# First attention of a two-layer kernel: projections as three fp32r products, the choice of experts one step later, the loop written out

## The chip, the cores and the metric

The kernel runs on one core of one Trainium2 chip. The metric is the device time of one execution in microseconds; less is better. The engines are named as the profile names them: PE (TensorE, matmuls), PEld (its weight loads), DVE (VectorE), ACT (ScalarE), POOL (GpSimd) and SP (SyncE, which only issues DMAs here).

## What is computed

The reference runs a transformer of two layers on x of 8 rows of 256 tokens with 128 features. Each layer has an attention and a feed-forward part, both behind a layer norm whose scale and shift come from a small conditioning vector. The change concerns the first attention and what follows it up to the experts' lists:

```python
h = _layernorm(x) * (1 + ca) + sa
q = (h @ w_q), kv = (h @ w_kv)          # 16 heads of 64: 128 -> 1024 columns
q, kv = rotated by position; q *= scale
# local keys: windows of 128 with the window before; global keys: softmax-pooled segments of 16
attn = softmax([global scores, local scores]); out = attn @ v
x = x + ga * (out @ w_out + b_out)
h = _layernorm(x) * (1 + cb) + sb
topk_vals, topk_idx = top_k(h @ router_w, 2)     # 4 experts
# the experts of layer 0 (fp32, 2730 hidden columns), then layer 1: another attention, 16 experts
```

## The kernel before, in words

Four stages run one after the other: layer0_attention, layer0_experts, layer1_attention, layer1_experts. Only the first is changed. It ends at about 590 us of the span.

**The pipeline of rows.** layer0_attention works on the 8 batch rows in steps that the code calls slots, from -2 to 8. In slot s the heads of row s are computed (`heads`), while row s+2 is normalised and its keys are projected and rotated (`norm`), row s+1 gets its key statistics, pooled segments and transposed keys (`early`), and row s-1 its output projection, residual, second layer norm, router and choice of experts (`late`). `parts` says which of these a slot has: slots 2 to 5 have all. Within a slot the loop runs over hp, 0 to 7, one pair of heads each ("pair 0" to "pair 7" below). Every engine has its own program of the same shape, slot_program, and all waits are written out by hand with semaphores. over_slots writes slots -2 to 1 and 6 to 8 out and puts slots 2 to 5 into a hardware loop of two turns.

**The heads.** For each pair PE computes the scores of pair n (L493 adds the mask, L498 the products), then the query projection of pair n+1 (q_proj, L481), then the attention-value product of pair n-2 (av, L526, L530) and the transposes of the probabilities of pair n-1 (pT_tr, L512, L514). DVE takes the reciprocal of the sums (L1021), the maximum of the scores (L1025), and rotates the queries of pair n+1 (L1081, L1085). ACT normalises the probabilities of pair n-1 (L648), takes the exponentials of pair n (L638), and copies the results of PE out (L701, L707, L708). A row's first scores wait for all its transposed keys, which ACT copies in pairs 6 and 7 (L661).

**What stands between them.** Pair 0: DVE reduces the logits (L851), centres keys (L835) and takes the statistics of the first layer norm of row s+2 (layernorm1, L761 to L769); PE transposes the logits at its end. Pair 1: segment softmax. Pair 2: on DVE segment_weights, kv_variance (L844, L846) and residual (L920 to L940); on PE the output projection (L539); POOL raises the variance to -0.5 (key_rstd, L1138) as soon as L846 is done, and then does weigh (L1160), normalise (L1147) and scale_keys (L1153). Pair 3: layernorm1_end (L806). Pair 4: PE transposes n2 and h (L547, L424), ACT writes hkv (L680) and h2T (L687), PE pools the segments (G_mm, L454) and projects the keys of half a row (kv_mm, L431); pair 5: the other half, the router matmul (L554), and on DVE pooled_variance (L903), kv_cosine (L818), router_rows (L950) and choose (L960 to L982), the choice of two experts for each token. Pair 6 and 7: rotation of the keys (L825, L827, L818 on DVE, L1127 and L1134 on POOL), key transposes (L471). At the end of pair 7 PE counts the places of row s-1 in the experts' lists (pos_mm, L562, L563), DVE makes them into indices (list_places, L987 to L1006), ACT copies hkv to hT (L737), and POOL scatters the rows to the lists with four indirect DMAs (L1230).

**The banks.** A0 and A1 are two PSUM banks that many small steps share. A string fixes the order of their uses in each slot, and each use waits until the one before is read out.

**Operands.** The projections are fp32 matmuls, each of which the trace shows as two records (PE) of two passes. The weights wq and wkv lie in SBUF as fp32, hT and hkv too. modb holds all six modulation vectors of every row, broadcast to 128 partitions.

## Time and profile before

| | |
|---|---|
| median of 3 runs | 1512.7 us (1509.84 to 1518.84) |
| profiled execution | 1513.62 us, span 1511.8 us |
| mean granted clock of TensorE | 0.896 |
| PE busy | 1200.5 us (79%) |
| DVE busy | 931.4 us (62%) |
| ACT busy | 822.3 us (54%) |
| POOL busy | 725.5 us (48%) |
| first scores of slot 0 | at 81.67 us |
| first rows read by the experts' stage | 594.35 us |

A timeline row of the profile has the start in us, the time in us from the first to the last of the merged instructions, the engine, the line, the operation with what it writes and reads, and their count; in brackets stands how long the engine was idle before and what ended that. A matmul's end is modelled with its way through the array, so a record's duration is longer than its distance to the next. The granted clock (PEclk) is 1.00 at 2.4 GHz and 0.50 at 1.2 GHz. A row of busy times has the stretch, its length, then busy us and, in parentheses, the instructions of PE, PEld, DVE, ACT and POOL, then PEclk, the share of the DMA engines and GB/s.

### The profile page before, as it was taken

To read this page: it belongs to the slowest core of one execution; us is meant where nothing else is said; L and a number is where in the kernel's file an instruction comes from. 1 tells how busy PE (TensorE), PEld (TensorE's weight loads), DVE (VectorE), ACT (ScalarE), POOL (GpSimd) and SP (SyncE) were. 2 spreads that over 40 slices of the span, in tenths; PEclk is the share of its full clock that TensorE was granted. 3 is DMA by queue.
4 is the path that set the end of the run, shared out by engine and by line. 5 is a ranking of instruction groups with operands and counts; after the bars stand their busy time and mean duration, and the time that the engine had idled before them with its cause. 6 is when DMAs were issued, how large, how long until landed. Compare 5 with 4: busy or idle time off the path is not lost. (4 is left out here: it accounts for less than half of the span.)

```text
span 1511.8 us, 30131 instructions
## 1 busy us (share of the span) xinstructions
PE 1200.5 (79%) x9299; PEld 928.5 (61%) x9299; DVE 931.4 (62%) x2122; ACT 822.3 (54%) x2181; POOL 725.5 (48%) x750
## 2 busy tenths in 40 slices
PE   3368988989889993898899899889937887888436
PEld 1245665656656662898899889889913444444336
DVE  4687787787876533744744664764434677776633
ACT  1256777767677771676676666666612443344101
POOL 2646748567485312565566556556653323211223
PEclk8589999989998995999999999999966999899558
DMA  7500000000000003303003000000063445331145
GB/s 221 174 2 3 1 10 3 8 10 0 9 2 8 10 8 127 124 11 125 8 11 120 16 9 10 12 12 7 10 174 81 84 87 104 58 48 21 23 121 152
DMA packets 152775, 76.43 MB, mean 51 GB/s; under 512 B 99992, under 2 KB 143384, under 8 KB 152408
## 3 DMA queue, kind: packets, MB, share of 16 engines
q1 hardware_dynamic: 144696, 66.42, 16.8%
q0 software_dynamic: 3072, 6.31, 1.3%
q10 hardware_dynamic: 4896, 2.36, 0.5%
q8 instruction: 54, 0.88, 0.2%
q14 instruction: 57, 0.47, 0.1%
HBM read 54.77 MB, written 19.76 MB: 49 GB/s over the span
## 5 line engine op out<-in xcount | busy, mean ns | idle before, releaser
L1477 POOL TENSOR_TENSOR hl<-hid,hh 128x256 fp32r<-128x256 f32 x396 | 294.0, 744 | 218.8 <-ACT hh L1454 215.1
L1520 DVE SCALAR_TENSOR_TENSOR hid<-GU,gub,sg 128x256 f32<-128x256 f32 x396 | 190.5, 482 | 194.7 <-ACT sg L1448 123.5
L1348 PE MATMUL GU<-xh,wh 128*128 128x256 f32 x792 | 233.3, 295 | 39.4 <-DVE wl L1496 30.3
L1448 ACT ACTIVATE sg<-GU,gub 128x256 f32<-128x256 f32 x396 | 188.1, 475 | 123.6 <-PE GU L1350 121.7
L1349 PE MATMUL GU<-xl,wh 128*128 128x256 f32 x792 | 225.3, 284 | 0.0
L1350 PE MATMUL GU<-xh,wl 128*128 128x256 f32 x792 | 225.1, 284 | 0.0
L1348 PEld LDWEIGHTS GU<-xh,wh 128*128 128x128 f32 x792 | 152.1, 192 | 49.0 <-issue 27.3
L1454 ACT CAST hh<-hid 128x256 fp32r<-128x256 f32 x396 | 158.2, 399 | 25.8 <-DVE hid L1520 25.3
L1349 PEld LDWEIGHTS GU<-xl,wh 128*128 128x128 f32 x792 | 152.5, 193 | 0.0
L1350 PEld LDWEIGHTS GU<-xh,wl 128*128 128x128 f32 x792 | 152.2, 192 | 0.0
L648 ACT ACTIVATE prob<-prob,rZ 128x272 f32<-128x272 f32 (+1 forms) x256 | 98.9, 462 | 60.6 <-DVE rZ L1021 55.2
L1961 ACT ACTIVATE pT<-ST 128x1024 f32<-128x1024 f32 x64 | 65.5, 1024 | 106.1 <-PE ST L1791 100.9
L1348 PE MATMUL OUT<-hh,wh 128*128 128x256 f32 x396 | 113.5, 287 | 10.8 <-ACT yT L1420 9.8
L2084 DVE TENSOR_REDUCE top_now<-S 128x4 f32<-128x1024 f32 x64 | 78.3, 1223 | 58.8 <-PE S L1783 50.6
L638 ACT ACTIVATE prob<-S,negmax 128x272 f32<-128x272 f32 (+1 forms) x256 | 106.6, 426 | 12.1 <-DVE negmax L1025 11.8
L1349 PE MATMUL OUT<-hl,wh 128*128 128x256 f32 x396 | 111.8, 282 | 0.0
L1350 PE MATMUL OUT<-hh,wl 128*128 128x256 f32 x396 | 111.7, 282 | 0.0
L1025 DVE TENSOR_REDUCE negmax<-S 128x2 f32<-128x544 f32 (+1 forms) x128 | 69.1, 581 | 67.7 <-PE S L498 64.6
L1783 PE MATMUL S<-KA,QA 32*128 32x256 f32 x512 | 81.2, 439 | 11.1 <-DVE top_now L2084 8.1
L1348 PEld LDWEIGHTS OUT<-hh,wh 128*128 128x128 f32 x396 | 75.3, 190 | 14.4 <-POOL hl L1477 13.6
L1138 POOL TENSOR_TENSOR krs<-krs,half 128x32 f32<-128x32 f32 x8 | 43.9, 5491 | 80.2 <-DVE krs L846 80.2
L1791 PE MATMUL ST<-QA,KA 32*128 32x256 f32 x512 | 78.8, 428 | 0.0
(312 smaller groups left out, 2842.6 us busy)
## 6 DMA issues: line engine op xcount, KB each, us to landing
raw<-in_expert_w SPq DMA_DIRECT2D x4, 2688.0 KB, 12.0
late<-in_w SPq DMA_DIRECT2D x20, 256.0 KB, 6.1
raw<-in_expert_w SPq DMA_DIRECT2D x4, 1152.0 KB, 6.1
list<-zero SPq DMA_DIRECT2D x4, 1024.0 KB, 8.6
modb<-mod_d SPq DMA_DIRECT2D x9, 384.0 KB, 4.3
early<-rel_d SPq DMA_DIRECT2D x1, 3072.0 KB, 13.1
qkv_d<-qkv SPq DMA_DIRECT2D x48, 64.0 KB
early<-in_w SPq DMA_DIRECT2D x12, 256.0 KB, 4.2
```

The source lines that it names most:

```text
L638: act.activation(prob[:, hp % 2, prob_at(t, e):prob_at(t, e) + KEYS[t]], S[:, e, S_AT[t]:S_AT[t] + KEYS[t]], ACT.Exp, bias=negmax[:, hp % ...
L648: i = act.activation(part, part, ACT.Copy, scale=rZ[:, pb, t, e:e + 1])
L1348: pe.matmul(out, lhs[0], rhs[0], start=start, stop=False, skip_group_check=True)
L1349: pe.matmul(out, lhs[0], rhs[1], start=False, stop=False, skip_group_check=True)
L1350: return pe.matmul(out, lhs[1], rhs[0], start=False, stop=stop, skip_group_check=True)
L1448: act.activation(sg[:, c % BUFS], GU[c % BUFS][:, 0:TT], ACT.Silu, bias=gub[:, GATE, e * CH0 + c:e * CH0 + c + 1]).then_inc(silu, 1)
L1454: act.copy(hh[:, d % BUFS], hid[:, d % BUFS]).then_inc(hid_hi, 1)
L1477: pool.tensor_tensor(hl[:, b], hid[:, b], hh[:, b].bitcast(F32), ALU.subtract).then_inc(hid_lo, 1)
L1520: dve.scalar_tensor_tensor(out=hid[:, c % BUFS], in0=GU[c % BUFS][:, TT:2 * TT], scalar=gub[:, UP, e * CH0 + c:e * CH0 + c + 1], in1=sg[:, ...
L1783: mm = pe.matmul(S[:, e, blk * NT:(blk + 1) * NT], QA[32 * j:32 * j + BLOCK, row % 2, g, blk * P:(blk + 1) * P], KA[32 * j:32 * j + BLOCK, ...
L1791: mm = pe.matmul(ST[:, e, blk * NT:(blk + 1) * NT], KA[32 * j:32 * j + BLOCK, row % 2, g, blk * P:(blk + 1) * P], QA[32 * j:32 * j + BLOCK ...
L2084: dve.tensor_reduce(to, S[:].rearrange("p e (q k) -> p e q k", q=2), X, ALU.max, negate=True).then_inc(s_max, 1)
```

## The change

Three things are done at once.

- **Split operands.** wq, wkv and the normalised input are each kept as a high part rounded to fp32r and a low part, the difference. A projection is three fp32r matmuls, high*high, high*low and low*high, into one accumulation (three), in place of one fp32 matmul. ACT makes the high parts (of wkv ahead of the slots, of wq in slot -1, of the input in pair 4 beside hkv), DVE the low ones (wkvl in slot -2, wql in slot -1, input_low in pair 4). The copy of hkv to hT goes. The fp32 weights share the memory of attT and pT.
- **One row later.** choose for row s-2 runs in pair 1 of slot s, its exponential on ACT there too, list_places and pos_mm in pair 2, the scatters at the head of the next slot, with two buffers for h2 and slot_now. pos_mm and its operands are bf16. The statistics of layernorm1 move from pair 0 to pair 4 of the slot before. A slot 9 is added for the last row's choice. The order in bank 0 has pos behind lgT.
- **Loops written out.** over_slots has no hardware loop any more, nor has SP's pooled_values. modb holds three of the six vectors.

```diff
@@ over_slots, parts @@
-def over_slots(eng, slot_program):
-    slot_program(-2, 0)
...
-    with eng.Fori(0, 2) as j:
-        slot_program(2 * j + 2, 0)
-        slot_program(2 * j + 3, 1)
-    for slot in range(6, NB + 1):
+def over_slots(slot_program):
+    for slot in range(-2, NB + 2):
         slot_program(slot, slot % 2)
@@ tiles @@
-        wq = sb("wq", [P, 2, INNER])
-        wkv = sb("wkv", [P, INNER])
+        wqh = sb("wqh", [P, 2, INNER], F32R)
+        wql = sb("wql", [P, 2, INNER], F32R)
+        wkvh = sb("wkvh", [P, INNER], F32R)
+        wkvl = sb("wkvl", [P, INNER], F32R)
-        modb = sb("modb", [P, NB, 6 * D])
+        modb = sb("modb", [P, NB, 3 * D])
-        hT = sb("hT", [P, 2, NT])
+        hTh = sb("hTh", [P, 3, NT], F32R)
+        hTl = sb("hTl", [P, 3, NT], F32R)
+        wq = attT[:].rearrange("p c q -> p (c q)").rearrange("p (s n) -> p s n", s=2)
+        wkv = pT[:].rearrange("p a e q -> p (a e q)")[:, 0:INNER]
-        h2 = sb("h2", [P, TILES, D])
+        h2 = sb("h2", [P, 2, TILES, D])
-        both = sb("both", [P, TILES, E0])
-        seen = sb("seen", [P, TILES + 1, E0])
+        both = sb("both", [P, TILES, E0], BF16)
+        seen = sb("seen", [P, TILES + 1, E0], BF16)
-        slot_now = sb("slot_now", [P, 2, TILES], U32)
+        slot_now = sb("slot_now", [P, 2, 2, TILES], U32)
-        bank0 = Bank(..., "lgT:E out:L h2T:L G:E kv00:N kv10:N kT1:E kT3:E pos:L")
+        bank0 = Bank(..., "lgT:E pos:M out:L h2T:L G:E kv00:N kv10:N kT1:E kT3:E")
@@ PE @@
+            def three(out, lhs, rhs):
+                pe.matmul(out, lhs[0], rhs[0], start=True, stop=False, skip_group_check=True)
+                pe.matmul(out, lhs[0], rhs[1], start=False, stop=False, skip_group_check=True)
+                return pe.matmul(out, lhs[1], rhs[0], start=False, stop=True, skip_group_check=True)
             def kv_mm(slot, t, n):
+                b = slot + 2
                 if t == 0 and n == 0:
-                    bank1.wait_emptied(pe, "hT", slot)
+                    pe.wait_ge(hq, b + 1)
+                    pe.wait_ge(w_low, 1)
                 bank, a = use(f"kv{t}{n}", slot)
-                pe.matmul(a[:], hkv[:, t * P:(t + 1) * P], wkv[:, n * 512:(n + 1) * 512],
-                          start=True, stop=True).then_inc(bank.full, 1)
+                tokens, cols = slice(t * P, (t + 1) * P), slice(n * 512, (n + 1) * 512)
+                three(a[:], (hTh[:, b % 3, tokens], hTl[:, b % 3, tokens]), (wkvh[:, cols], wkvl[:, cols])).then_inc(bank.full, 1)
             def q_proj(n, b, bp, hp):
                 if hp == 0:
                     pe.wait_ge(hq, b + 1)
+                    pe.wait_ge(w_low, 2)
...
                 for s in range(2):
-                    mm = pe.matmul(Q[:, s * NT:(s + 1) * NT], wq[:, s, hp * P:(hp + 1) * P], hT[:, bp, :],
-                                   start=True, stop=True)
+                    mm = three(Q[:, s * NT:(s + 1) * NT], (wqh[:, s, cols], wql[:, s, cols]), (hTh[:, b % 3, :], hTl[:, b % 3, :]))
             def pos_mm(slot, b):
-                    pe.matmul(a[:, t * E0:(t + 1) * E0], cst("before"), both[:, t, :], start=True, stop=False)
-                    mm = pe.matmul(a[:, t * E0:(t + 1) * E0], cst("ones"), seen[:, t, :], start=False, stop=True)
+                    pe.matmul(a[:, t * E0:(t + 1) * E0], beforeb[:], both[:, t, :], start=True, stop=False)
+                    mm = pe.matmul(a[:, t * E0:(t + 1) * E0], onesb[:], seen[:, t, :], start=False, stop=True)
@@ PE, slot_program: behind scores, in front of the next projection @@
                     if heads:
                         scores(n, slot, bp, hp)
+                    if slot > 1 and hp == 2:
+                        pos_mm(slot, slot - 2)
...
-                    if late and hp == 7:
-                        pos_mm(slot, slot - 1)
@@ ACT @@
+            act.wait_ge(w_in, 16 * n_w)
+            act.copy(wkvh[:], wkv).then_inc(w_high, 1)
...
+                        if r >= 1:
+                            act.wait_ge(hq, r)
+                        if r >= 3:
+                            act.wait_ge(q_mm, HP * (r - 2))
-                        act.activation(hkv[:], A1[:, 0:NT], ACT.Identity, ...).then_inc(bank1.drained, 1)
+                        for to in (hTh[:, r % 3, :], hkv[:]):
+                            i = act.activation(to, A1[:, 0:NT], ACT.Identity, ...)
+                        i.then_inc(bank1.drained, 1)
...
-                    if late and hp == 6:
-                        act.wait_ge(t_step, T_STEPS * l + 4)
+                    if slot > 1 and hp == 1:
+                        act.wait_ge(t_step, T_STEPS * (slot - 2) + 4)
                         act.activation(ew[:, 1, :], ew[:, 0, :], ACT.Exp).then_inc(t_exp, 1)
-                    if norm and hp == 7:
-                        if not known_zero(r - 1):
-                            act.wait_ge(q_mm, HP * (r - 1))
-                        act.copy(hT[:, bp, :], hkv[:]).then_inc(hq, 1)
+                    if slot == -1 and hp == 3:
+                        act.wait_ge(wq_in, 16 * n_wq)
+                        act.copy(wqh[:], wq).then_inc(w_high, 1)
@@ DVE @@
+            def input_low(slot, r):
+                bank1.wait_emptied(dve, "hT", slot)
+                dve.tensor_tensor(hTl[:, r % 3, :], hkv[:], hTh[:, r % 3, :].bitcast(F32), ALU.subtract).then_inc(hq, 1)
...
-                    if norm and hp == 0 and not (isinstance(slot, int) and slot == -2):
-                        layernorm1(r)
                     if early and hp == 1:
                         segment_softmax(slot, b)
+                    if slot > 1 and hp == 1:
+                        choose(slot - 2)
+                    if slot > 1 and hp == 2:
+                        list_places(slot, slot - 2)
                     if early and hp == 2:
                         segment_weights(b)
                         kv_variance(b)
...
+                    if slot == -2 and hp == 3:
+                        dve.wait_ge(w_high, 1)
+                        dve.tensor_tensor(wkvl[:], wkv, wkvh[:].bitcast(F32), ALU.subtract).then_inc(w_low, 1)
+                    if norm and hp == 4:
+                        input_low(slot, r)
+                    if slot < NB - 3 and hp == 4:
+                        layernorm1(r + 1)
                     if early and hp == 4:
                         pooled_norm(slot, b)
+                    if slot == -1 and hp == 5:
+                        dve.wait_ge(w_high, 2)
+                        dve.tensor_tensor(wql[:], wq, wqh[:].bitcast(F32), ALU.subtract).then_inc(w_low, 1)
                     if early and hp == 5:
                         pooled_variance(b)
                     if norm and hp == 5:
                         kv_cosine(slot, r, 0)
                     if late and hp == 5:
                         router_rows(slot, l)
-                        choose(slot, l)
...
-                    if late and hp == 7:
-                        list_places(slot, l)
@@ POOL @@
+            def to_lists(b):
+                pool.wait_ge(h2_done, 2 * (b + 1))
+                pool.wait_ge(slot_out, 2 * (b + 1))
...
+                        pool.indirect_dma_start(io["list0"], ...slot_now[:, b % 2, k, t:t + 1]..., h2[:, b % 2, t, :], None).then_inc(scat[b % 2], 16)
...
+                    if slot > 2 and slot <= NB and hp == 0:
+                        to_lists(slot - 3)
+                    if slot == NB and hp == 5:
+                        to_lists(NB - 2)
+                    if slot == NB + 1 and hp == 2:
+                        to_lists(NB - 1)
```

## Rows read from the trace of the kernel before

**Rows 1.** Busy times by stretch: slots 3, 4 and 7 of the pipeline.

```profile
264.94:327.12 62.18, 54.75 (x367) 38.09 (x368) 49.80 (x108) 45.13 (x138) 40.27 (x27) 0.94 0.02 7
327.12:391.01 63.89, 57.27 (x367) 39.34 (x368) 49.70 (x108) 44.88 (x138) 40.30 (x27) 0.90 0.02 6
...
509.34:556.00 46.66, 43.75 (x320) 31.85 (x321) 23.71 (x81) 37.98 (x127) 6.32 (x8) 1.00 0.02 7
```

**Rows 2.** Timeline of PE: pairs 4 to 7 of slot 3, head of slot 4.

```profile
299.72 1.88 PE L431 MATMUL A<-wkv,hkv 128*128 128x512 f32 x4
301.44 0.46 PE L493 MATMUL S<-maskb,identb 128*128 128x288 bf16 x2
...
302.83 1.13 PE L481 MATMUL Q<-hT,wq 128*128 128x256 f32 x4
303.80 0.51 PE L554 MATMUL A<-rw,h2T 128*128 128x4 f32 x4
...
315.65 0.46 PE L493 MATMUL S<-maskb,identb 128*128 128x288 bf16 x2
...
322.59 0.55 PE L512 MATMUL PT<-const,prob 128*128 128x128 f32 x3 [2.11 <-ACT prob L648]
...
325.40 0.58 PE L562 MATMUL A<-both,const 128*128 128x4 f32 x2 [1.70 <-ACT kT L661]
...
327.12 0.75 PE L493 MATMUL S<-maskb,identb 128*128 128x288 bf16 x2
...
329.67 2.07 PE L481 MATMUL Q<-hT,wq 128*128 128x256 f32 x4
```

**Rows 3.** Busy time of two short stretches, columns as in rows 1.

```profile
204.00:208.00 4.00, 4.00 (x16) 2.29 (x14) 3.79 (x16) 2.52 (x9) 1.50 (x2) 0.51 0.02 7
...
324.00:336.00 12.00, 10.60 (x42) 7.30 (x42) 8.60 (x19) 6.35 (x21) 6.28 (x5) 0.50 0.07 23
```

**Rows 4.** Timeline of DVE: slot 3 from pair 5, and pair 6 of slot 7.

```profile
308.03 0.15 DVE L950 COPY rl<-A 128x8 f32<-128x8 f32 x1
...
311.68 0.18 DVE L1021 RECIPROCAL rZ<-Z 128x4 f32<-128x4 f32 x1
...
317.51 3.35 DVE L818 TENSOR_TENSOR kvr<-kvraw,const 128x1024 f32<-128x1024 f32 x1
320.79 0.17 DVE L1021 RECIPROCAL rZ<-Z 128x4 f32<-128x4 f32 x1
...
327.55 0.15 DVE L987 SCALAR_TENSOR_TENSOR pos<-const,A 128x8 f32<-128x8 f32 x1
...
332.09 0.18 DVE L1021 RECIPROCAL rZ<-Z 128x4 f32<-128x4 f32 x1 [2.99 <-issue]
...
543.03 0.16 DVE L950 COPY rl<-A 128x8 f32<-128x8 f32 x1
...
545.16 0.16 DVE L982 TENSOR_TENSOR seen<-seen,both 128x4 f32<-128x4 f32 x1
```

**Rows 5.** Busy time of a stretch of layer0_experts, columns as in rows 1.

```profile
650.00:700.00 50.00, 47.47 (x396) 46.72 (x395) 22.22 (x47) 34.35 (x91) 31.42 (x44) 1.00 0.26 97
```

**Rows 6.** Single lines: duration in ns min/median/max, first and last start.

```profile
L1500 DVE TENSOR_TENSOR xl<-XT,xh x19: 424/425/425, 595.6 to 1096.6; 128x256 fp32r<-128x256 f32 x19
...
L818 DVE TENSOR_TENSOR kvr<-kvraw,const x16: 1211/1894/3358, 27.3 to 443.7; 128x1024 f32<-128x1024 f32 x16
...
L721 ACT ACTIVATE kvs<-kvc x16: 1056/1070/1109, 42.4 to 469.0; 128x1024 f32<-128x1024 f32 x16
```

**Rows 7.** Timeline of POOL: slot -1, pairs 2 and 6 of slot 3.

```profile
57.80 3.76 POOL L1147 TENSOR_TENSOR V<-kvc,krs 128x1024 f32<-128x1024 f32 x2
...
285.69 5.54 POOL L1138 TENSOR_TENSOR krs<-krs,half 128x32 f32<-128x32 f32 x1 [10.00 <-DVE krs L846]
...
317.43 2.35 POOL L1134 TENSOR_TENSOR wk<-kvr,wproj 128x1024 f32<-128x1024 f32 x1
```

**Rows 8.** Timeline of PE behind the last head of row 7.

```profile
577.21 0.59 PE L562 MATMUL A<-both,const 128*128 128x4 f32 x2 [2.40 <-DVE seen L982]
```

133 lines of the change are left out of this document (62 added, 71 removed).

## The prediction

> **What bounds the kernel now.** I read first the busy times by row of the pipeline [rows 1]. A full row (slots 2 to 5) takes 62.2 us, the fourth 63.9. In it PE is busy 55 to 57 us, DVE 50, ACT 45, POOL 40: PE looks like the bound, but the granted clock of slot 4 is 0.90, so part of that busy time is PE at half speed. The timeline of PE [rows 2] shows where. Pairs 1 to 6 run almost without a gap; the last pair of the row starts at 315.65 and the next row at 327.12: 11.47 us, where pair 3, which has nothing beside the heads' own work, takes 4.9. PE stands 2.11 us for ACT's normalised scores, then 1.70 us in front of the matmuls that count the experts' places. Behind it the clock falls: in 324 to 336 us it is 0.50 [rows 3], 1.2 GHz, and four records of a query projection show 2.07 us where they show 1.13 at 2.4 GHz [rows 2]. The timeline of DVE [rows 4] says why PE stood: DVE has no gap from kv_cosine in pair 5 to the end of the row. The choice of experts takes it 3.65 us (308.03 to 311.68), the list of places 1.4 us (327.55 to 328.94), and kv_cosine, 1.21 us at its shortest [rows 6], takes 3.35 us beside POOL. So the row's end is bound by DVE, its middle by PE, and pair 4 by a chain through ACT and POOL. Last, the loop: DVE stands 2.99 us on "issue" between slots 3 and 4 and nowhere else at a row's edge.
>
> **The products.** Before, one pair of query projections is 4 records, 0.97 us from its start to the next instruction (302.83 to 303.80), and two key projections are 4 records, 1.72 us (299.72 to 301.44) [rows 2]. The experts' stage has the new form already: 396 records of it, nearly all 128x256 fp32r, fill 47.5 us, 0.12 each [rows 5]. Six of them are 0.72 us: 0.25 less per pair, 2.0 per row. A key projection has 512 columns, so twice that less overhead, 0.21 to 0.24 a record: 6 are 1.3 to 1.45, 0.3 to 0.4 less per two, 0.7 per row. The count of places falls from 8 fp32 records at half clock (1.72 us, 325.40 to 327.12) to 4 small bf16 ones, 0.3 to 0.5. PE's work shrinks by some 3.5 us a row, but only where PE is what is waited for. New beside them: input_low on DVE, 0.42 us [rows 6], and on ACT a second activation of 0.45 us for a copy of 0.45 that goes; the first makes PE wait for ACT, then DVE. In slot 3 hkv is done at 295.8, DVE leaves the query rotation at 297.9, and PE reaches the key projections at 299.7: hidden, with 1.4 us to spare. If the cover went, it would cost at most 1 us a row.
>
> **A full row, pair by pair,** on the times of slot 3 [rows 2, 4]. *Pair 5* keeps its length but for 0.3: its second half waits for DVE's copy of the router rows, and that does not move. *Pair 6*: without the choice DVE takes the maximum when PE's scores are done, 310.4 instead of 311.77, 1.4 us sooner. Its kv_cosine then reaches the port ahead of POOL's 2.35 us product [rows 7], so 1.1 us more: the reciprocal of 320.79 comes at 318.3. *Pair 7*: ACT's key copies, which the next row's scores wait for, end 2.3 us sooner (323.0), and the place matmuls are gone: the next row starts at 323.1, not 327.1. The pair shrinks from 11.47 to 8.05. *Pair 0*: DVE is free at 325.3; maximum and rotation 2.2, logits 2.34, and PE's transpose waits for them: 330.2, so 7.1 against 8.2. *Pair 1*: the layer norm (1.1 us) is gone from DVE, 4.5 against 5.2. Here the choice comes back, though, behind the rotation: beside an idle POOL it is 2.3 us, as in slot 7 (543.03 to 545.3 [rows 4]), where beside a busy POOL it is 3.65. DVE ends it at +7.1 of the pair, 2.6 us into pair 2. *Pair 2*: PE stands in its new place for the choice (1.1 us, and the projection of the next pair is queued behind it), DVE has 1.3 us of places more in front of the 2.3 us variance and the 2.8 us residual: 9.7 against 8.7. *Pair 3*: DVE comes 3.0 us late instead of 1.4, so ACT normalises late and PE waits: 6.3 against 4.9. *Pair 4*: n2 and h2T, 0.5 us later, 10.0 against 9.5. The sum is -3.4 -1.1 -0.7 +1.0 +1.4 +0.5 -0.3 -0.2 = -2.8, a row of 59.4 us.
>
> That is at full clock. PE still stands 0.7 and 1.9 us in pair 7 and 2.2 in pair 0, and at the end of slot 1 stalls of no more were followed by 0.51 [rows 3]. If it falls as before, pair 0 is PE's again and 2.2 us longer: gain 0.6 a row. I take the middle, 1.7, over four rows 6.8, and both ends for the range (2.4 to 11.2).
>
> **The rest of the sum.** The loop's edge: slot 4 is 63.89 us, the others within 0.2 of 62.2, and DVE's 2.99 us lie in its first pair: 1.8 us go with the loop [rows 1, 4]. Slot 1 loses the choice and gets none back: 3.5. Slot 0 has no choice; PE's shorter products where POOL isn't waited for: 1.5. Slot 6 has no new row to prepare; less at its end, the give-back as above: 2.0. Slot 7 is PE's (43.75 of 46.66 us [rows 1]): seven projections at 0.25 and the places, 2.2. Behind the last head PE's places (577.21 to 579.1) shrink by 1.1 [rows 8]; the choice for row 6, its list and its four scatters (5 us of POOL) fall into waits of DVE and POOL for the last output projection, and POOL's modulation is still done before the last list. Earlier scatters move to the head of a row, where POOL is idle more than 4 us. Halved broadcasts on SP are waited for by nobody.
>
> The start pays. In slot -2 the first key projection (22.77) now waits for ACT's copy of wkv (about 1.06, as a 128x1024 activation [rows 6]), DVE's difference (1.22) and input_low: +1.9; the products are shorter and layernorm1 leaves a full DVE: net +0.3. In slot -1 DVE gets the difference of wq, 128x2048, twice 1.2 = 2.4 us, in the stretch in which POOL's chain from 57.8 to 77.0 has no gap and sets the first scores [rows 6, 7]. What it costs the trace doesn't show: nothing, if both run side by side; 2.4 if POOL waits for it; 5 if DVE waits for a product of POOL's as well and its variance comes late to POOL. I take 2.2, nearest to the rows in which the two delay each other, so +2.5 in all.
> The Trainium skill (SBUF — State Buffer, Who interferes with whom) has it that a VectorE instruction with two SBUF inputs and a GpSimd one that reads SBUF exclude each other whole; the trace agrees, 3.35 us against 1.21 beside a product of 2.35 [rows 4, 6, 7]. By it the start costs +2.4; by a mere sharing of bandwidth it would be nearer nothing.
>
> Sum: +2.5 -1.5 -3.5 -6.8 -1.8 -2.0 -2.2 -1.1 = -16.4. Against the profiled execution's own 1513.6 (span 1511.8 and 1.8 around it) that is 1497; it lies 0.9 above the median of the runs shown, 1512.7. I say 1498.
>
> **Rivals.** *The clock holds.* If the shorter stalls at the rows' ends let PE stay at 2.4 GHz, four rows give 2.8 each, slot 6 another 2, and pairs 1 to 3 give back less with PE's shorter work: 1513 - 29 = 1484. For it: slot 6, which prepares no row, ended with shorter stalls and slot 7 has 1.00 [rows 1]. Against: slot 1's end, which did not keep it. *Only moved.* DVE's work per row is the same, 50 us and 0.42 more, and what it no longer does at the end it does in pairs 1 and 2: if PE's stall moves whole from pair 7 to pairs 2 to 4 and the clock falls there, what is left is slot 1, the loop's edge and slot 7, less the start: 1513 - 5 = 1508. *Slower.* The place is DVE's variance in pair 2, which releases POOL's 5.5 us power and with it POOL's gapless 34 us chain [rows 7]. It comes about 2 us later in the row (9.4 after the pair's start, 7.3 now). My walk lets pair 4 take it up in PE's wait; if POOL's chain is instead what pairs 4 to 7 hang on, each of five late rows gets 2 us longer than now and gives nothing at its end, and with 5 at the start that is +15 less 3: 1525. It decides where POOL's product of wk ends later than ACT's h2T; now it is half a microsecond before it, so little is missing. Against it: POOL stands 4.4 us later in the row. A fourth: unrolled code could stall on instruction loads at every row. The trace has none in the written-out slots, 2.99 us at the jump.
> The Trainium skill (Runtime: NRT & Kernel Launch, Instruction fetch mechanics) says that a taken branch breaks sequential prefetch and straight code doesn't; the trace's one gap at the jump agrees.
>
> **How the numbers follow.** Forecast 0.55 (own range 1488 to 1506), clock holds 0.17, only moved 0.18, slower 0.10. The range 1480 to 1512 leaves out the slow case and the far half of the fast one. 0.5%, about what a measurement of this kernel can tell, is 7.6 us: below 1505 lie nearly all of the forecast, the fast case and a little of the third: 0.73. Within it 0.18, slower 0.09.
>
> **What would show it.** Rows of 59 to 61.5 us in the busy times by row; the last pair of a row 8 us with no wait in front of places; the longest idle of DVE no longer at 2.99 "issue"; pair 2 and 3 longer by 1 each; projections at 0.12 us a record. First scores at 84 instead of 81.7. The forecast is wrong if pairs 2 to 4 grow by more than 4 us, if the clock at the rows' heads is 1.00, or if POOL's wk becomes PE's longest wait.

## The result, and the profile after

The changed kernel takes 1511.23 us at the median of 14 runs (1499.61 to 1526.53), the kernel before 1518.18 in 14 runs (1509.62 to 1527.67). The ratio is 0.9942, 95% interval 0.9917 to 0.9966: faster by about 0.6%, roughly 9 us by the ratio and 7 by the medians, where 16.4 were forecast. The median lies inside the range (1480 to 1512), at its slow end. Part of the distance to the 1498 of the forecast is its starting value: 1512.7 was the median of 3 runs, and 14 runs of the same kernel give 1518.2. The profiled execution of the changed kernel took 1516.29 us (span 1514.4, mean clock 0.880), 5 above its own median; that of before lay 4.6 below its own. The spans of the two profiles therefore say nothing of the change, and what follows reads the first attention alone. It ends where PE reads the first rows for the experts (XT<-const,rows): at 594.35 us before, at 591.70 after, and at 586.36 in a second profile of the changed kernel (r_after below).

Each row of the pipeline starts with the mask matmul of its first pair. From these starts in the two timelines of PE:

| stretch | before, us | after, us | difference | forecast |
|---|---|---|---|---|
| up to the first scores | 81.67 | 84.98 | +3.3 | +2.5 |
| slot 0 | 60.17 | 60.71 | +0.5 | -1.5 |
| slot 1 | 60.97 | 60.92 | 0.0 | -3.5 |
| slots 2, 3 | 62.13, 62.18 | 61.88, 61.87 | -0.3 each | -1.7 each |
| slot 4, with the loop's edge | 63.89 | 63.62 | -0.3 | -3.5 |
| slot 5 | 62.28 | 59.00 | -3.3 | -1.7 |
| slot 6 | 56.05 | 55.63 | -0.4 | -2.0 |
| slot 7, seven pairs | 40.03 | 39.28 | -0.8 | -2.2 |
| from there to the experts' first rows | 44.98 | 43.81 | -1.2 | -1.1 |
| sum | | | -2.7 | -16.4 |

Only the tail and slot 5 gave what was forecast, or more. The second profile has 61.62, 59.58, 60.66, 62.04 and 59.72 us for slots 1 to 5, so a row's length is known to about 2 us from one profile. Busy times of the changed kernel, slots 3, 4 and 5, the answer to [rows 1]:

```profile
268.49:330.36 61.87, 53.48 (x382) 39.68 (x383) 48.43 (x109) 45.33 (x139) 42.68 (x28) 0.92 0.02 7
330.36:393.98 63.62, 55.21 (x383) 40.77 (x384) 48.64 (x109) 45.67 (x139) 42.84 (x28) 0.89 0.02 7
393.98:452.98 59.00, 52.42 (x383) 38.30 (x384) 47.10 (x104) 45.37 (x139) 42.83 (x28) 0.94 0.02 7
```

Slot 5 differs from 3 and 4 in one thing: there is no next row, so DVE has 104 instructions instead of 109. The five missing ones are the layer norm in pair 4. Here are the pairs of slot 3, from the same starts (us):

| pair | 0 | 1 | 2 | 3 | 4 | 5 | 6 | 7 |
|---|---|---|---|---|---|---|---|---|
| before | 8.16 | 5.27 | 8.71 | 4.87 | 9.49 | 7.76 | 6.45 | 11.47 |
| after | 7.96 | 5.15 | 10.27 | 4.66 | 13.68 | 6.55 | 5.78 | 7.82 |
| forecast, clock held | 7.1 | 4.5 | 9.7 | 6.3 | 10.0 | 7.5 | 6.3 | 8.1 |

The last pair shrank as forecast; pair 4 took it back. The timeline of PE in the changed kernel (start, duration, instruction; in brackets the wait before it and what ended it) answers to [rows 2] and [rows 8]:

```profile
285.46 3.81 PE L536 MATMUL A<-wout,attT 128*128 128x128 f32 x32 [1.40 <-DVE pos L995]
...
293.28 0.39 PE L398 MATMUL Q<-hTh,wqh 128*128 128x256 f32 x1
293.50 0.28 PE L399 MATMUL Q<-hTl,wqh 128*128 128x256 f32 x1
...
294.18 0.69 PE L523 MATMUL O<-pT,gv 32*128 32x256 f32 x2
...
301.51 1.10 PE L450 MATMUL A<-wk,const 128*32 128x256 f32 x16 [1.52 <-ACT h2T L692]
...
307.51 0.77 PE L398 MATMUL A<-wkvh,hTh 128*128 128x512 f32 x1 [2.45 <-DVE gc L904]
308.07 0.63 PE L399 MATMUL A<-wkvl,hTh 128*128 128x512 f32 x1
...
327.51 0.55 PE L509 MATMUL PT<-const,prob 128*128 128x128 f32 x3 [0.30 <-ACT prob L648]
...
330.36 0.46 PE L490 MATMUL S<-maskb,identb 128*128 128x288 bf16 x2 [1.76 <-ACT kT L661]
...
430.91 0.47 PE L398 MATMUL A<-wkvh,hTh 128*128 128x512 f32 x1 [0.24 <-DVE gc L904]
431.21 0.40 PE L399 MATMUL A<-wkvl,hTh 128*128 128x512 f32 x1
...
576.21 0.19 PE L559 MATMUL A<-both,beforeb 128*128 128x4 bf16 x1 [3.97 <-DVE seen L990]
```

To be seen: six records of a query projection take 0.90 us (293.28 to 294.18), of which the first has 0.22. In pair 4 of slot 3 PE stands 1.52 us for h2T (0.74 before, the row below), works 3.5 us, stands 2.45 us for gc, and then sends its first two key records 0.56 us apart; in slot 5 the same wait is 0.24 us and they stand 0.30 apart. In front of the row's last probabilities PE waits 0.30 us where it waited 2.11, and at its end 1.76 for ACT's keys. The kernel before, pair 4 of slot 3:

```profile
296.34 1.09 PE L454 MATMUL A<-wk,const 128*32 128x256 f32 x16 [0.74 <-ACT h2T L687]
```

The windows give the granted clock (third number from the end), to set beside [rows 3]:

```profile
307.00:311.00 4.00, 3.49 (x10) 2.24 (x12) 0.45 (x2) 1.56 (x4) 1.87 (x1) 0.57 0.00 0
...
334.00:338.00 4.00, 4.00 (x18) 2.58 (x18) 3.86 (x5) 2.61 (x11) 3.21 (x4) 0.50 0.14 49
431.00:435.00 4.00, 4.00 (x28) 3.17 (x28) 1.11 (x3) 3.60 (x9) 4.00 (x3) 1.00 0.00 0
```

In this profile the clock now falls in pair 4 as well as at the row's head. The timeline of DVE says why gc is late: start of slot -1, pair 4 of slots 3 and 5, and the last choice.

```profile
61.56 3.29 DVE L1077 TENSOR_TENSOR wql<-attT,wqh 128x2048 fp32r<-128x2048 f32 x1
...
280.80 0.21 DVE L968 MAX8 top<-rl 128x8 f32<-128x8 f32 x2
...
282.64 0.18 DVE L1029 RECIPROCAL rZ<-Z 128x4 f32<-128x4 f32 x1
...
302.23 2.12 DVE L818 TENSOR_TENSOR hTl<-hkv,hTh 128x256 fp32r<-128x256 f32 x1
304.27 0.47 DVE L765 BATCH_NORM_STATS2 bn<-xt 128x6 f32<-128x128 f32 x2
...
305.17 1.41 DVE L773 TENSOR_SCALAR rs<-mv 128x2 f32<-128x2 f32 x1
306.50 0.41 DVE L902 TENSOR_REDUCE gst<-A 128x4 f32<-128x256 f32 x1
306.94 0.42 DVE L904 SCALAR_TENSOR_TENSOR gc<-gst,A 128x256 f32<-128x256 f32 x1
...
427.85 2.12 DVE L818 TENSOR_TENSOR hTl<-hkv,hTh 128x256 fp32r<-128x256 f32 x1
...
430.34 0.42 DVE L904 SCALAR_TENSOR_TENSOR gc<-gst,A 128x256 f32<-128x256 f32 x1
...
573.67 0.86 DVE L981 TENSOR_TENSOR hot<-const,topf 128x8 f32<-128x8 f32 x2
```

And POOL at the same times:

```profile
62.66 7.79 POOL L1172 TENSOR_TENSOR V<-V,lng 128x1024 f32<-128x1024 f32 x2
...
290.00 5.44 POOL L1157 TENSOR_TENSOR krs<-krs,half 128x32 f32<-128x32 f32 x1 [12.83 <-DVE krs L854]
...
300.13 3.94 POOL L1166 TENSOR_TENSOR V<-kvc,krs 128x1024 f32<-128x1024 f32 x2
304.03 4.84 POOL L1172 TENSOR_TENSOR V<-V,lng 128x1024 f32<-128x1024 f32 x2
...
574.41 0.73 POOL L1200 TENSOR_TENSOR h<-n,modb 128x256 f32<-128x256 f32 x1
```

From 302.23 to 307.28 DVE has no gap: input_low (2.12 beside POOL's products, 0.42 at the shortest of its eight), the layer norm of the row after (2.23 from 304.27 to 306.50, of which rs is 1.41), and only then gst and gc of pooled_norm. In bank 0 the first key projection stands behind G, the tile that gc reads; so PE waits.

### The profile page after: what moved, and what is told of

Read it like the earlier page. It is cut to its first block and busy times, and to the rows that moved or that the text cites. A ratio compares the mean times of both kernels' runs of the same rounds, so it can differ in the third digit from the quotient of the medians.

```text
span 1514.4 us, 29868 instructions
## 1 busy us (share of the span) xinstructions
PE 1191.7 (79%) x9426; PEld 942.0 (62%) x9426; DVE 932.6 (62%) x2134; ACT 826.6 (55%) x2183; POOL 742.1 (49%) x750
## 5 line engine op out<-in xcount | busy, mean ns | idle before, releaser
L1810 PE MATMUL S<-KA,QA 32*128 32x256 f32 x512 | 82.1, 443 | 12.5 <-DVE top_now L2111 10.0
L1375 PEld LDWEIGHTS OUT<-hh,wh 128*128 128x128 f32 x396 | 75.4, 190 | 14.4 <-POOL hl L1504 13.5
L1818 PE MATMUL ST<-QA,KA 32*128 32x256 f32 x512 | 82.6, 445 | 0.0
```

The costliest lines, as they stand in the source:

```text
L1375: pe.matmul(out, lhs[0], rhs[0], start=start, stop=False, skip_group_check=True)
L1810: mm = pe.matmul(S[:, e, blk * NT:(blk + 1) * NT], QA[32 * j:32 * j + BLOCK, row % 2, g, blk * P:(blk + 1) * P], KA[32 * j:32 * j + BLOCK, ...
L1818: mm = pe.matmul(ST[:, e, blk * NT:(blk + 1) * NT], KA[32 * j:32 * j + BLOCK, row % 2, g, blk * P:(blk + 1) * P], QA[32 * j:32 * j + BLOCK ...
```

## The experiments

Stage end is the start of XT<-const,rows in the run's profile. Each line has 5 to 12 runs and one profile, in three groups, each beside its own runs of the kernel before (medians 1518.42 for r_after, e1, e3 and e4; 1521.97 for e5 to e8; 1519.57 for e2 and e9 to e11). The times carry the verdicts. A stage end comes from one profile, and two of them lie 5.3 us apart for the changed kernel alone; that of e1_ln_behind was taken in its longest run, 1510.49 us.

| run | median us | ratio, 95% | stage end | pair 4 in slots 2, 3, 4 |
|---|---|---|---|---|
| r_after, the changed kernel again | 1509.69 | 0.9957 (0.9924 to 0.9990) | 586.36 | 12.45, 12.45, 13.81 |
| e1_ln_behind | 1500.68 | 0.9858 (0.9827 to 0.9889) | 583.01 | 10.25, 12.78, 9.76 |
| e3_fp32_products | 1519.34 | 1.0005 (0.9981 to 1.0029) | 599.78 | 12.68, 12.67, 12.74 |
| e4_choice_back | 1517.79 | 0.9990 (0.9965 to 1.0015) | 601.14 | 13.64, 14.19, 12.98 |
| e5_places_pair3 | 1498.35 | 0.9845 (0.9810 to 0.9879) | 570.06 | 9.75, 10.66, 9.76 |
| e6_h2T_first | 1498.81 | 0.9854 (0.9815 to 0.9894) | 577.11 | 10.23, 10.24, 9.58 |
| e7_all | 1490.81 | 0.9807 (0.9765 to 0.9850) | 573.44 | 9.13, 10.65, 9.13 |
| e8_unrolled | 1515.48 | 0.9966 (0.9935 to 0.9997) | 587.06 | 9.62, 9.63, 9.62 |
| e2_ln_pair0 | 1501.46 | 0.9887 (0.9855 to 0.9920) | 580.22 | 10.24, 10.24, 12.75 |
| e9_ln_behind_fp32 | 1503.71 | 0.9891 (0.9861 to 0.9921) | 587.26 | 10.45, 10.45, 10.52 |
| e10_start_tail | 1503.73 | 0.9905 (0.9871 to 0.9939) | 588.69 | 12.46, 12.45, 12.74 |
| e11_choice_back_ln_behind | 1510.04 | 0.9938 (0.9916 to 0.9960) | 588.29 | 10.74, 10.75, 10.74 |

### The changed kernel once more

> The changed kernel again, beside the experiments on the same chip. Both theories: ratio to the kernel before 0.99 to 1.00; rows (slots 1 to 4) of 61 to 63.6 us and slot 5 of 59.0; pair 4 at 13.5 us in slots 1 to 4 and 10.2 in slot 5; the experts' stage reads its first rows at 591.7 us. If the profile's longer second attention (more half clock after 1350 us) was chance, it is not there again.

0.9957, as expected. The trace is the same in its waits, but not in its clock: slots 1 to 4 take 61.62, 59.58, 60.66 and 62.04 us, and pair 4 is 12.45 in slots 2 and 3 and 11.36 in slot 5, where 13.5 and 10.2 were expected. The stage ended 5.3 us earlier than in the first profile of the same program. In slot 2:

```profile
239.37 1.09 PE L450 MATMUL A<-wk,const 128*32 128x256 f32 x16 [1.52 <-ACT h2T L692]
...
245.38 0.47 PE L398 MATMUL A<-wkvh,hTh 128*128 128x512 f32 x1 [2.46 <-DVE gc L904]
```

```profile
245.00:249.00 4.00, 3.62 (x24) 2.82 (x25) 0.96 (x3) 2.96 (x7) 3.00 (x3) 1.00 0.00 0
```

The two waits are those of the first profile, and here the clock held at 1.00 behind them and at the row's head too (pair 0 7.23). So the wait and the fall of the clock can be priced apart: pair 4 is 10.23 us without the layer norm at full clock (slot 5 of the first profile), 12.45 with it at full clock, 13.68 with it and the clock fallen behind it. In slot 3 of this profile the clock fell before, behind the wait for h2T; the wait for gc was then 0.91 instead of 2.46 and the pair 12.45 all the same, so that a fall there hides in the wait.

### The layer norm behind pooled_norm

```diff
+                    if early and hp == 4:
+                        pooled_norm(slot, b)
                     if slot < NB - 3 and hp == 4:
                         layernorm1(r + 1)
-                    if early and hp == 4:
-                        pooled_norm(slot, b)
```

> One edit to the changed kernel: in pair 4 DVE takes layernorm1 of the next row behind pooled_norm instead of in front of it. Theory 1 (the gain was lost in pair 4, because the first key projection waits in bank 0 for pooled_norm, which stands behind 2.1 us of layer-norm statistics on DVE, and the clock falls on that wait): pair 4 falls from 13.5 to 10.2 us in slots 1 to 4 as in slot 5, the rows are 58.5 to 59.5 us, the first attention ends 10 to 15 us sooner, about 578 to 581 us. Rival (the longer pair 4 comes from the products' new operands, input_low and ACT's second activation, or from POOL's later chain): pair 4 stays at 12.5 us or more and the end moves by less than 4 us.

The swap of two calls makes the changed kernel faster by 9.0 us by the medians, 15 by the ratios, and the intervals of the two ratios don't touch. DVE and PE in pair 4 of slot 2:

```profile
239.52 2.12 DVE L818 TENSOR_TENSOR hTl<-hkv,hTh 128x256 fp32r<-128x256 f32 x1
241.56 0.41 DVE L902 TENSOR_REDUCE gst<-A 128x4 f32<-128x256 f32 x1
242.01 0.42 DVE L904 SCALAR_TENSOR_TENSOR gc<-gst,A 128x256 f32<-128x256 f32 x1
242.34 0.48 DVE L765 BATCH_NORM_STATS2 bn<-xt 128x6 f32<-128x128 f32 x2
```

```profile
242.57 0.48 PE L398 MATMUL A<-wkvh,hTh 128*128 128x512 f32 x1 [0.24 <-DVE gc L904]
242.89 0.40 PE L399 MATMUL A<-wkvl,hTh 128*128 128x512 f32 x1
```

The wait for gc is 0.24 instead of 2.45 and the key records are at full clock. Not all rows keep it: in slots 1 and 3 PE doesn't wait for gc at all, but the clock falls behind the 1.52 us for h2T (0.50 from 298.66 to 304.66), and pair 4 is 11.38 and 12.78. The time bears the theory out; the stage end, 3.3 and 8.7 us before those of the changed kernel's two profiles, would have left the rival open.

### The layer norm in pair 0 of the row before

```diff
+                    if norm and hp == 0 and slot > -2:
+                        layernorm1(r)
...
-                    if slot < NB - 3 and hp == 4:
-                        layernorm1(r + 1)
```

> The changed kernel, with the layer norm of the next row's input moved from pair 4 to pair 0 of the row before it is needed (slot -2 keeps its own place). Theory (in pair 4 anything that stands on DVE ahead of pooled_norm is waited for by the first key projection, and the clock falls there): pair 4 of the full rows is 10 to 10.8 us where it is 13.5 in the changed kernel, as in the kernel with the layer norm behind pooled_norm, but the 1.1 us now stand in front of DVE's rotation at a row's head, so pair 0 gets 1 to 2 us longer; ratio to the kernel before 0.986 to 0.991. Rival (what helped was only that layer norm and reciprocal no longer stand in pair 4 beside POOL's power): the ratio equals that of the kernel with the layer norm behind pooled_norm, 0.9858, or is below it.

Pair 4 is 10.24 in slots 2 and 3 as expected, but 12.75 and 12.94 in slots 4 and 5, where the clock falls behind the wait for h2T as in e1_ln_behind. Pair 0 is 7.23 to 8.42 us in slots 2 to 5 where e1_ln_behind has 7.22 in three of them and 7.97 in the fourth; in both kernels it is 7.2 where the clock held, so the 1 to 2 us more of the theory aren't there. The ratio lies in the range of the theory, but its interval still holds the rival's 0.9858: this run doesn't tell the two apart. It shows that the other place, too, beats the one ahead of pooled_norm.

### One product instead of three

```diff
-                pe.matmul(out, lhs[0], rhs[0], start=True, stop=False, skip_group_check=True)
-                pe.matmul(out, lhs[0], rhs[1], start=False, stop=False, skip_group_check=True)
-                return pe.matmul(out, lhs[1], rhs[0], start=False, stop=True, skip_group_check=True)
+                return pe.matmul(out, lhs[0].bitcast(F32), rhs[0].bitcast(F32), start=True, stop=True)
```

The products with the low parts are left out; their operands are still made.

> The changed kernel with each of the three fp32r products of a projection replaced by one fp32 matmul of the high parts; the low parts are still made and waited for, but their products are left out. It measures the term for PE's products alone. Theory 1: the products give 0.25 us a pair only where PE is waited for, pairs 1 and 3 and all of slot 7: 8 to 12 us longer in the first attention than the changed kernel, of which about 2 in slot 7. Rival (PE's work is hidden behind DVE and ACT in all full rows): under 4 us longer.

> The changed kernel with the layer norm behind pooled_norm and, in place of three products of split operands, one fp32 product of the high parts (the products with the low parts are left out, their operands are still made). If the split products are worth what they were with the layer norm ahead (10 us), the ratio is 0.992 to 0.993 against 0.9858 with them, and rows are 1.3 to 2 us longer. If they were only worth it because they shortened the half-clock stretch behind the wait in pair 4, they are worth 3 to 5 us here and the ratio is 0.988.

With the layer norm ahead the split products are worth 9.7 us by the medians and 7 by the ratios (1.0005 against 0.9957); with it behind, 2 (each against its own runs of before) and 5 (0.9891 against 0.9858). The intervals of these differences are as wide as the differences. The stage end of e3_fp32_products is 8.1 and 13.4 us behind those of the changed kernel's two profiles, about the 8 to 12 expected, but the time is not lost where it was expected: pairs 1 and 3 grow by 0.16 us each and slot 7 by 1.0. Nor do the half-clock stretches of pair 4 explain it: there the clock is 1.00 in slots 1 to 5, and pair 4 no longer than in the changed kernel. It is the last pair that has 9.68 us instead of 7.82 in slots 1 to 4. Slot 3 of e3_fp32_products, DVE, POOL and PE:

```profile
328.68 3.35 DVE L824 TENSOR_TENSOR kvr<-kvraw,const 128x1024 f32<-128x1024 f32 x1
```

```profile
328.60 2.35 POOL L1151 TENSOR_TENSOR wk<-kvr,wproj 128x1024 f32<-128x1024 f32 x1
```

```profile
312.35 1.95 PE L398 MATMUL A<-wkvh,hTh 128*128 128x512 f32 x4 [2.35 <-DVE gc L902]
...
333.75 0.55 PE L507 MATMUL PT<-const,prob 128*128 128x128 f32 x3 [2.01 <-ACT prob L646]
```

kv_cosine (kvr<-kvraw) begins 0.08 us behind POOL's product, takes 3.35 us, and PE waits 2.01 us for the probabilities. In the changed kernel it begins 1.16 us ahead of that product, takes 2.28, and PE waits 0.30. With the layer norm behind, it is ahead with either kind of product (last pair 7.64 and 7.82). So by these profiles most of what the split products are worth with the layer norm ahead is this order of two instructions, four times 1.86 us. The rest is 0.16 us a projection, and heads of rows of 9.0 to 9.2 us instead of 7.4 to 8.5.

### The choice of experts back in its own row

```diff
-  "lgT:E pos:M out:L h2T:L G:E kv00:N kv10:N kT1:E kT3:E"
+  "lgT:E out:L h2T:L G:E kv00:N kv10:N kT1:E kT3:E pos:L"
...
                         router_rows(slot, l)
+                        choose(l)
...
+                    if late and hp == 7:
+                        list_places(slot, l)
```

(pos_mm on PE, the exponential on ACT and the scatters on POOL go back likewise; e11 has the layer norm behind pooled_norm besides.)

> The changed kernel with the choice of experts, its places and the scatters back in the row's pairs 5 and 7; the fp32r products, the written-out loop and the place of layernorm1 stay. Theory 1: pair 7 goes back from 7.8 to about 11 us and pair 2 from 10.4 to 8.5, pair 4 keeps its 13.5; rows of about 63 to 64, the end 6 to 9 us later than the changed kernel's. Rival (the choice was only moved, its gain at the row's end is all given back in pair 2 and behind): within 3 us of the changed kernel.

> The changed kernel with the layer norm behind pooled_norm, and the choice of experts, the places and the scatters back in the same row (pairs 5 and 7). With the layer norm ahead the same edit cost 8 us (1517.8 against 1509.7). If the choice's later place is worth the same by itself, the ratio is 0.991 to 0.992 against 0.9858, with the last pair of a row at 9 us and the next row's head at half clock. If the later choice mainly costs what pairs 2 and 3 give back, the ratio stays within 0.003 of 0.9858.

The move one row later is worth 8.1 us by the medians, 5 by the ratios, with the layer norm ahead, and 8 to 12 with it behind (0.9938 against 0.9858). In e4_choice_back the last pair is 9.03, where about 11 was expected. Slot 3 of e11_choice_back_ln_behind:

```profile
267.28:328.84 61.56, 53.83 (x384) 39.26 (x383) 51.71 (x109) 45.21 (x139) 40.52 (x28) 0.92 0.02 7
```

Its last pair is 9.03 and its first 8.94 us, where e1_ln_behind has 7.82 and 7.22. The row has the new products and is no shorter than those of the old kernel with its loop written out (61.39, below). What the products gain, 0.16 in pair 2 and 0.6 in the last, is taken back in pair 4 (10.75 against 9.63), where the split operands are made, and in pair 0 at a clock of 0.50 (8.94 against 8.19).

### The loop alone

The kernel before, with nothing but the rows written out.

```diff
-    slot_program(-2, 0)
...
-    with eng.Fori(0, 2) as j:
-        slot_program(2 * j + 2, 0)
-        slot_program(2 * j + 3, 1)
-    for slot in range(6, NB + 1):
+    for slot in range(-2, NB + 1):
```

> The kernel before with nothing changed but the hardware loop over slots 2 to 5, which is written out on all engines. Theory: the first pair of slot 4 falls from 9.99 to 8.2 us and the first attention ends 1 to 2.5 us sooner than 594.35, ratio 0.998 to 0.9995. Rival (written-out code stalls on its loads, or the loop's edge was covered): no change or later.

Slots 3 and 4:

```profile
263.60:324.99 61.39, 54.88 (x369) 38.37 (x369) 49.64 (x108) 44.93 (x139) 40.34 (x28) 0.94 0.02 6
324.99:386.35 61.36, 54.87 (x369) 38.33 (x368) 49.50 (x108) 44.91 (x139) 40.25 (x28) 0.94 0.02 7
```

Slot 4 loses 2.5 us, its first pair falls from 9.99 to 8.18 as expected, and DVE has no "issue" gap of over 0.4 us in the stage any more. Slots 2, 3 and 5, which had no such gap, are 0.8 to 1.1 shorter too. DVE and PE in the last pairs of slot 3:

```profile
317.14 2.35 DVE L811 TENSOR_TENSOR kvr<-kvraw,const 128x1024 f32<-128x1024 f32 x1
```

```profile
321.21 0.55 PE L505 MATMUL PT<-const,prob 128*128 128x128 f32 x3 [1.05 <-ACT prob L641]
```

In the loop kv_cosine begins 0.08 us behind POOL's product and takes 3.35 us [rows 4, 7]; here it begins 1.09 behind and takes 2.35, as in slot 1 of the kernel before, which was written out there too. PE waits 1.05 us for the probabilities instead of 2.11, with two short waits in pair 6 in exchange (0.48 and 0.83), and the places' matmuls take 0.89 instead of 1.72 us, at full clock. Pair 6 is 1.0 longer, the last 1.8 shorter: 9.66 instead of 11.47. Why the order differs inside the loop, no run shows. The ratio, 0.9966, is 5 us (0.5 to 10): by its middle about half of what the whole change brought.

### The places one pair later

On top of e1_ln_behind:

```diff
-  "lgT:E pos:M out:L h2T:L G:E kv00:N kv10:N kT1:E kT3:E"
+  "lgT:E out:L pos:M h2T:L G:E kv00:N kv10:N kT1:E kT3:E"
...
-                    if slot > 1 and hp == 2:
+                    if slot > 1 and hp == 3:
                         pos_mm(slot, slot - 2)
```

(and list_places on DVE likewise, behind the residual).

> The kernel with layernorm1 behind pooled_norm, and besides the places of the experts (their matmuls on PE and list_places on DVE) in pair 3 instead of pair 2, with their use of bank 0 behind the output projection's. Theory: pair 2 is 1.6 us longer than before because the output projection waits 1.41 us in bank 0 for DVE's places, and in most rows the clock now falls in pair 2 or 4 on the sum of these waits. Pair 2 falls from 10.3 (12.2 at half clock) to 8.6, pair 3 rises from 4.66 to about 5.1; the first attention ends 6 to 10 us before the 583 of the kernel without this edit. Rival (DVE's backlog simply appears in pair 3 and 4): less than 3 us.

Pair 2 of slot 3, and the places in pair 3, on PE:

```profile
274.58 3.73 PE L536 MATMUL A<-wout,attT 128*128 128x128 f32 x32
...
282.32 0.18 PE L559 MATMUL A<-both,beforeb 128*128 128x4 bf16 x1
```

Neither waits. Pair 2 is 8.5 us in slots 2 to 6, where the changed kernel has 10.3 to 10.9, and pair 3 is 4.8 to 4.9. In its profile the stage ends 13 us before that of e1_ln_behind; in the times the two can't be told apart (0.9845 and 0.9858).

### h2T first on ACT

On top of e1_ln_behind, ACT's copy of h2T stands ahead of those of hTh and hkv in pair 4.

> The kernel with layernorm1 behind pooled_norm, and besides ACT writes h2T before hTh and hkv in pair 4. Theory: the second activation for the split input is not free, it stands in front of h2T, for which PE's segment pooling waits 1.52 us in every full row (0.74 before the change). Pair 4 falls by 0.7 to 1.0 us in slots 1 to 5, and the end comes 4 to 6 us sooner than 583, or more where the clock holds. Rival (POOL's product of weights, and not ACT, releases the pooling, since POOL's chain starts later): no change in pair 4.

0.9854: no different from e1_ln_behind. PE in pair 4 of slot 3:

```profile
294.32 1.09 PE L450 MATMUL A<-wk,const 128*32 128x256 f32 x16 [0.62 <-ACT h2T L681]
...
299.01 0.48 PE L398 MATMUL A<-wkvh,hTh 128*128 128x512 f32 x1 [1.14 <-DVE gc L904]
```

The wait for h2T falls from 1.52 to 0.62 and that for gc rises from 0.24 to 1.14: the same 1.76 in all. Neither the theory nor its rival (POOL's product) was right. What sets the pair is DVE's list, also with the layer norm out of it.

### The start and the tail

```diff
-                    if slot == -1 and hp == 5:
+                    if slot == -1 and hp == 3:
                         dve.wait_ge(w_high, 2)
                         dve.tensor_tensor(wql[:], wq, wqh[:].bitcast(F32), ALU.subtract).then_inc(w_low, 1)
...
-                    if slot == NB and hp == 5:
-                        to_lists(NB - 2)
...
                         modulate(l)
+                    if slot == NB and hp == 5:
+                        to_lists(NB - 2)
```

> The changed kernel with two edits outside the full rows: DVE takes the difference of the second weight in pair 3 of the first slots instead of pair 5, and in the last slot POOL's modulation stands ahead of the list of the row before. Theory: the first scores come at 82.5 instead of 84.98 (the difference of 2048 columns no longer stands beside POOL's gapless chain), and PE waits 2.4 us instead of 3.97 for the last choice; full rows as in the changed kernel, pair 4 near 13.5. Together 3 to 4 us, ratio 0.992 to 0.993. Rival (the start's 3.3 us come from the first key projection alone): first scores stay within 0.5 us of 84.98.

```profile
82.47 0.46 PE L490 MATMUL S<-maskb,identb 128*128 128x288 bf16 x2 [3.10 <-DVE qr L1102]
...
573.21 0.19 PE L559 MATMUL A<-both,beforeb 128*128 128x4 bf16 x1 [2.42 <-DVE seen L990]
```

The first scores and the last wait are as expected, to a tenth. 0.9905 against 0.9957 is 8 us where 3 to 4 were expected, the intervals overlapping; pair 4 is 12.5 to 12.7. The profile's stage end, 588.69, shows no gain: its clock fell in the last head of all, behind a wait that the changed kernel has as well, and the tail is 46.15 us long for 43.81.

### All of them

e1_ln_behind with the places in pair 3, h2T first, the weight's difference early and the tail's two calls swapped.

> All edits together: layernorm1 behind pooled_norm, places in pair 3, h2T first, the difference of wq on DVE in pair 3 of slot -1 (beside POOL's power, where DVE is idle) instead of pair 5, and in slot 8 POOL's modulation of the last row in front of the scatters of the row before. Theory: rows of 56 to 58 us, first scores at 82 instead of 85, the first attention ends at 562 to 572 us, ratio to the kernel before 0.975 to 0.983. Rival (one wait is only traded for the next): the end stays above 577, ratio over 0.984.

1490.81 us, 0.9807: the fastest, ahead of both kernels by more than the intervals, with the ratio inside its range and the stage end, 573.44, just behind its own. The lead over e5_places_pair3 is 0.4% with overlapping intervals. Its rows are not even: slots 2 and 4 take 56.15 and 57.65, slots 3 and 5 both 61.85, with 8.6 us in pairs 0 and 1 each. There PE waited 1.76 for prob and 1.62 for lg, and the clock is 0.50 behind them; which rows are spared stays open.

## Why the prediction was right and wrong

**The direction and the last pair: right, the last pair in part by luck.** Pair 7 was to shrink to 8.05 us and is 7.82; the wait in front of the places is gone, that for prob 0.30, and kv_cosine goes ahead of POOL's product as the walk had it. But the walk gave all of this to the choice, and 1.8 us of it come with the written-out loop alone (9.66 in e8_unrolled). Pairs 6 and 7 together are 17.92 us before, 17.14 with the loop alone written out, 16.60 with the products besides (slot 2 of e4_choice_back), and 13.60 in the changed kernel: the move is 3.0 of the 4.3. **The products: oversized.** The records are 0.12 us as taken from the experts' stage, but the first of six takes 0.22. A pair gains 0.16 us where 0.25 was forecast (pair 3 is 4.82 in the old kernel written out and 4.66 in the changed one), 1.3 a row instead of 2.0. The slower rival (POOL's chain) didn't come: POOL's power starts 21.5 us into slot 3 (290.00), 20.75 before, and no wait for wk became PE's longest.

**The step that failed is pair 4 of the walk,** "n2 and h2T, 0.5 us later, 10.0 against 9.5", together with "hidden, with 1.4 us to spare" for input_low. The walk followed ACT, and left DVE's list for that pair out: input_low took 2.12 us, not 0.42; the layer norm, which I had taken off pair 1 as a gain of 0.7, came back here with 2.23 us; and PE's first key projection waits in bank 0 for the gc behind both. That wait is 2.45 us, and the granted clock behind it was 0.57, so pair 4 cost 4.2 us in slot 3 instead of 0.5, and 3.5 to 4 in slots 1, 2 and 4. Of the 4.2, 0.8 stay without the layer norm (10.24 against 9.49: the split operands, near the forecast 0.5), 2.2 are the layer norm's wait at full clock (12.45), and 1.2 the clock (13.68). Pairs 2 to 4 grew by 5.5 us in slot 3: that is the prediction's own sign of being wrong, "by more than 4 us". Slot 5, which has no layer norm, gained 3.3. The swap that takes only the layer norm out of the way took the wait to 0.24 and brought 9 to 15 us: with it the ratio of the change is 0.9858, where the forecast had 0.989. No run moves input_low by itself; with the layer norm out of the way PE waits for what stands behind it 0.24 us or not at all. The same term explains slot 1, which had pair 4 at 13.66 for 9.63, and its 3.5 us forecast that never came.

**The choice in pairs 1 and 2: size right, wait wrong.** Pair 2 grew by 1.6 in slot 3, forecast 1.0. But DVE needs only 1.84 us for the choice beside an idle POOL (280.80 to 282.64), and the choice is in time in slot 3 and 0.2 and 0.5 us late in slots 4 and 5. What PE waits 1.40 us for is DVE's reading of the counted places: in bank 0 they stand ahead of the output projection. I had named the choice itself, and not counted this on slot 7, where pair 2 grew by 1.6 us too (8.37 to 9.97), about what slot 7 lacks of its forecast; with the order changed it is back at 8.5. Pair 3 was to be 1.4 longer and is 0.2 shorter: DVE is not late there, it waits 0.85 us for PE's scores (293.38).

**The clock at the rows' heads: about right, as the middle of two ends.** It fell at every head of slots 2 to 5 in the first profile of the changed kernel; in the second it held at slot 2. Where it held, pairs 0 and 1 are 7.23 and 4.65, that is 11.9 us; where it fell they are 12.6 to 14.3, on average 1.3 us more. The walk had 11.6 for them and a fall at 2.2; the middle that I took, 1.1 us a row, is near the measured 1.3. So this term didn't fail, and the missing 1.4 us a row is not at the heads. The rival in which the clock always holds is refuted. In e1_ln_behind it holds at the heads of slots 2, 3, 4 and 6, but falls in pair 1 or 2 of each of these rows. The condition was not the last pair alone.

**The loop: undersized.** 1.8 us forecast from slot 4 alone; 5 by the experiment, of which 2.5 are in slot 4, where the 2.99 us on "issue" delayed DVE. The other rows of the loop gain 0.8 to 1.1 each, which the forecast didn't have: kv_cosine and POOL's product meet in another order there, PE's stall is cut into shorter ones, and 0.8 us are the places' matmuls at full clock. In the changed kernel's own slot 4 pair 4 hides the gain.

**The start: mechanism right.** 3.3 us against 2.5. The difference of wq was taken for 2.4 us, with a cost of 2.2; it took 3.29, POOL's two products beside it 7.79 where they took 5.62 before, and moved two pairs earlier it let the first scores come 2.5 us sooner. Each delays the other, and the middle value was too kind by little. **The tail** was right in sum (-1.2) and wrong in its parts: POOL's modulation was to be done before the last list, but it stood behind the four scatters of row 6 and ran beside the last row's choice (574.41), where hot took 0.86 us instead of 0.24, and PE waited 3.97 us instead of 2.40; the places' matmuls, 0.3 us for 1.9 until DVE reads them, paid for it.

"Only moved" was the rival nearest to what happened: it had 1508 from 1513, that is 5 us, with the stall going to pairs 2 to 4 and the clock falling there. What it counted as left over, slot 1 and the loop's edge, gave nothing, so its number is near by luck. Its chance, 0.18, was too small, because I priced pair 4 without writing down what stands in each engine's queue there.

The Trainium skill (SBUF — State Buffer, Who interferes with whom) lists which VectorE instructions share a port with GpSimd: those with two SBUF inputs, and tensor_scalar where it can enter a two-port mode; not a reduction, nor, outside such modes, one with a single SBUF input. The trace agrees in each case: hTl 2.12 for 0.42, rs 1.41 for 128x2, but the reduction gst 0.41 and gc, whose one 128x256 input is in PSUM, 0.42 beside a product of POOL as well. Read against the list of pair 4 ahead of time, it would have said which of its instructions can be held up; for how long, only the trace shows.

## What to carry to other kernels

Where a step is moved or added, write out what then stands on each engine between the last input and the instruction that PE waits for, and look up which tile stands ahead of that one in its PSUM bank: here a swap of two calls was worth as much as the whole change or more (9 to 15 us against 7 to 9). Price VectorE work of two SBUF inputs by what GpSimd does at that moment, not by its shortest record. Undo or do each part alone: about half of this gain was the loop, and what looked like the price of a matmul was for the most part the order in which two other engines' instructions met.

## What was not expected of the hardware

- A tensor_scalar on two elements per partition took 1.41 us beside POOL's product (305.17) and 0.66 in e1_ln_behind (243.25), where another one, of four elements, takes 0.17 in the changed kernel with POOL idle (314.38). Both long ones end as one product of POOL ends and the next begins (306.52 and 243.84): they last as long as what is left of it.
- The clock falls behind waits none of which is over 2.5 us, and not always: 1.52 and 2.45 us in pair 4 gave 0.57 in slot 3 of the changed kernel, and 1.52 and 2.46 gave 1.00 in slot 2 of its second profile. 1.36 and 2.35 gave 1.00 in slot 3 of e3_fp32_products. 1.52 alone gave 0.50 in slot 3 of e1_ln_behind, and 1.00 in its slot 4.
- In pair 4 the fall costs about what the wait for gc does, and the two overlap: 10.24 us without either, 12.45 with the wait, 12.75 with the fall alone (slot 4 of e2_ln_pair0), 12.45 to 13.68 with both.
- The part behind the stage, which no run here changed, took 915 to 927 us in the profiles. One profile can't show a gain of 10 us here; pair lengths repeated over rows can. What decides which rows keep their clock stays open.
